# Weight preparation software-pipelined by three chunks, and moved behind the first projection

## The reference, cut to what matters

```python
# x: (32, 2048, 1024) fp32; four batches to a core
xn = layernorm(x)
x + attn(xn) + ffn(xn)

def attn(xn):                       # 16 heads of 64
    q, k, v = xn @ Wq + bq, xn @ Wk + bk, xn @ Wv + bv
    q_freq, k_freq, v_freq = rfft over the sequence of q, k, v
    idx = top 64 frequencies by mean |q_freq|
    score = sum(q.real * k.real) / 8 at idx;  attn = softmax(score)
    out_freq = mean over frequencies of q_freq, with attn * v.real put at idx
    return irfft(out_freq) @ Wo + bo

def ffn(xn):                        # int32 weights, scale 1/127, hidden 3072
    return (silu(xn @ wg.T) * (xn @ wu.T)) @ wd.T
```

## Time and profile before

| what | us |
|---|---|
| three timed runs | 5865.82, 5973.41, 6274.16 |
| their median | 5973.41 |
| the profiled execution's own time | 5865.05 |
| its span (slowest core, first to last instruction) | 5863.5 |
| the spans of its 8 cores | 5843.6 to 5863.5 |
| TensorE busy | 4717.2 (80%) |
| VectorE, ScalarE, GpSimd busy | 1368.9, 837.2, 60.7 |

### The profile page before, as it was taken

One profiled execution on the slowest core, in us unless ns is written; L12 is line 12 of the kernel. 1 busy time (PEld: TensorE's weight loads), 2 busy tenths in 40 slices (PEclk: granted clock), 3 DMA queues, 4 the chain that ended last, 5 costly groups with the idle time before them and its releaser, 6 DMA issues.

```text
span 5863.5 us, 52343 instructions; the slowest of 8 cores (5843.6 to 5863.5 us)
## 1 busy us (share of the span) xinstructions
PE 4717.2 (80%) x20720; PEld 1989.3 (34%) x20720; DVE 1368.9 (23%) x1819; ACT 837.2 (14%) x976; POOL 60.7 (1%) x116
## 2 busy tenths in 40 slices
PE   0157468899885898799995799789987599889989
PEld 0023123344332333234442343234433243324434
DVE  1113023112122322202222232302222332221212
ACT  1111011122101111022201111112200111112210
POOL 0000000000000000000000000000000000000000
PEclk9778778999996999899997799899998799989999
DMA  3232222122341211222242211213233031212234
GB/s 98 86 90 79 75 61 72 42 85 76 110 126 52 61 44 36 76 68 77 63 154 85 47 44 46 66 56 88 76 120 121 29 72 44 55 51 81 79 99 124
DMA packets 570711, 441.87 MB, mean 75 GB/s; under 512 B 276940, under 2 KB 473676, under 8 KB 570472
## 3 DMA queue, kind: packets, MB, share of 16 engines
q1 hardware_dynamic: 548712, 360.92, 22.2%
q0 software_dynamic: 12544, 44.05, 2.3%
q10 hardware_dynamic: 9216, 33.56, 1.4%
HBM read 373.46 MB, written 65.01 MB: 75 GB/s over the span
## 4 chain that ended last, share of the span: by engine, by line
PE 75%; DMA 13%; DVE 6%; issue 3%; ACT 2%; DVEq 0%; ACTq 0%; SPq 0%; POOLq 0%
PE pw L587 14%; PE pw L917 11%; PE pw L926 11%; PE pw L958 11%; PE pw L469 8%; PE pw L541 4%; PE pw L827 4%; PE pw L860 4%; DMA strm<-wq_s 1%; PE pw L477 1%; DMA strm<-wv_s 1%; DMA r<-wdT_s 1%; PE pw L631 1%; DMA wdT_s<-spE 1%; DVE msum L499 1%
## 5 line engine op out<-in xcount | busy, mean ns | idle before, releaser
L587 PE MATMUL pw<-r,strm 128*128 128x512 bf16 x4096 | 922.7, 389 | 195.7 <-ACT r L595 156.3
L917 PE MATMUL pw<-r,strm 128*128 128x512 bf16 x3072 | 703.2, 382 | 36.2 <-ACT strm L901 36.2
L469 PE MATMUL pw<-strm,r 128*128 128x512 bf16 x2304 | 541.5, 388 | 211.8 <-ACT r L481 188.1
L926 PE MATMUL pw<-r,strm 128*128 128x512 bf16 x3072 | 694.4, 379 | 0.0
L587 PEld LDWEIGHTS pw<-r,strm 128*128 128x128 bf16 x4096 | 407.8, 100 | 709.0 <-issue 250.4
L958 PE MATMUL pw<-r 128*128 128x512 bf16 x2048 | 459.9, 383 | 63.3 <-DMA r<-wdT_s 63.3
L936 DVE TENSOR_TENSOR r<-strm,pw 128x1024 bf16<-128x1024 bf16 x192 | 234.5, 1221 | 1036.1 <-PE pw L926 1036.1
L917 PEld LDWEIGHTS pw<-r,strm 128*128 128x128 bf16 x3072 | 302.4, 99 | 406.3 <-issue 50.0
L926 PEld LDWEIGHTS pw<-r,strm 128*128 128x128 bf16 x3072 | 300.6, 98 | 362.5
L469 PEld LDWEIGHTS pw<-strm,r 128*128 128x128 bf16 x2304 | 216.3, 99 | 527.2 <-issue 300.7
L933 ACT ACTIVATE strm<-pw 128x1024 bf16<-128x1024 f32 x192 | 196.6, 1024 | 1015.2 <-PE pw L917 1015.1
(11 more groups left out here) (173 smaller groups left out, 2662.1 us busy)
## 6 DMA issues: line engine op xcount, KB each, us to landing
strm<-dft_cos SPq DMA_DIRECT2D x96, 512.0 KB
r<-x SPq DMA_DIRECT2D x64, 512.0 KB
spA<-wg SPq DMA_DIRECT2D x48, 512.0 KB
spC<-wu SPq DMA_DIRECT2D x48, 512.0 KB
spB<-wg SPq DMA_DIRECT2D x48, 512.0 KB
spD<-wu SPq DMA_DIRECT2D x48, 512.0 KB
strm<-dft_sinn SPq DMA_DIRECT2D x32, 512.0 KB
r<-crt SPq DMA_DIRECT2D x8, 2048.0 KB
```

What stands on the lines that cost most here:

```text
L469: e.matmul(pw[pwi][:, eta * 512:(eta + 1) * 512], xnT[:, dc, tau * 128:(tau + 1) * 128], wv[:, dc, eta * 512:(eta + 1) * 512], start=(dc = ...
L587: e.matmul(pw[pwi][:, eta * 512:(eta + 1) * 512], slotv[:, tau, :], sig[:, tau, eta * 512:(eta + 1) * 512], start=(tau == 0), stop=(tau == ...
L917: e.matmul(pw[pg][:, tq * 512:(tq + 1) * 512], wgv[:, dc, :], xnT[:, dc, th * 1024 + tq * 512:th * 1024 + (tq + 1) * 512], start=(dc == 0) ...
L926: e.matmul(pw[pu][:, tq * 512:(tq + 1) * 512], wuv[:, dc, :], xnT[:, dc, th * 1024 + tq * 512:th * 1024 + (tq + 1) * 512], start=(dc == 0) ...
```

## The change

It has two parts. First, `prep_one` still emits the load at once, but puts cast and store of the chunk on a list; when the list holds more than three, the oldest pair is emitted. So the cast and the store of chunk i are emitted behind the load of chunk i + 3. `prep_flush` emits the last three pairs at the end of each weight of eight chunks and of each group of twelve. The fences stay: POOL still waits for every DMA to land before it issues the next. Second, the preparation of Wk and Wv is emitted after the first projection and not before it.

```diff
+    prep_pipe = []
...
         em("g", lambda e, it=it, src_ap=src_ap:
            e.dma_start(out=it, in_=src_ap), writes=SP4[par], dma=True)
-        em("v" if i % 2 == 0 else "s", lambda e, it=it, ph=ph, i=i:
-           (e.tensor_copy if i % 2 == 0 else e.copy)(spEh[ph], it),
-           reads=SP4[par], writes=[f"spE{ph}"])
-        em("g", lambda e, ph=ph, dst_ap=dst_ap: e.dma_start(out=dst_ap, in_=spEh[ph]),
-           reads=[f"spE{ph}"], writes=[dtk], dma=True)
+
+        def cast_store(i=i, it=it, par=par, ph=ph, dst_ap=dst_ap, dtk=dtk):
+            em("v" if i % 2 == 0 else "s", lambda e, it=it, ph=ph, i=i:
+               (e.tensor_copy if i % 2 == 0 else e.copy)(spEh[ph], it),
+               reads=SP4[par], writes=[f"spE{ph}"])
+            em("g", lambda e, ph=ph, dst_ap=dst_ap: e.dma_start(out=dst_ap, in_=spEh[ph]),
+               reads=[f"spE{ph}"], writes=[dtk], dma=True)
+
+        prep_pipe.append(cast_store)
+        if len(prep_pipe) > 3:
+            prep_pipe.pop(0)()
+
+    def prep_flush():
+        while prep_pipe:
+            prep_pipe.pop(0)()
 
     def prep_attn(nm):
         for dc in range(8):
             prep_one(W_ins[nm][dc * 128:(dc + 1) * 128, :],
                      w_scr[nm][dc * 128:(dc + 1) * 128, :], f"scr{nm}", False)
+        prep_flush()
...
         prep_state["i"] = min(i0 + n, len(ffn_chunks))
+        prep_flush()
...
             phase_ln(b)
+            phase_proj(b, 0)
             prep_attn("Wk")
             prep_attn("Wv")
-            phase_proj(b, 0)
             prep_attn("Wo")
```

## The result

Over ten runs each, the changed kernel takes 0.9866 of the time of the kernel before (95% interval 0.9853 to 0.9880): a small gain, clear of the noise. This ratio leaves out the runs in which one die was granted a lower clock, which the medians over all ten, 5843.0 and 5871.13 us, mix in. The forecast was 5781 / 5865.05 = 0.9857. The profiled execution took 5789.06 us, its span is 5787.5 (before 5863.5): 76.0 us less, where the sum gave 84.1.

What follows compares the result with a forecast made beforehand. TensorE, 80% busy, was taken to stand still behind POOL's weight preparation, whose casts precede the PSUM evictions. Terms -17.3 - 14.4 - 26.2 - 26.2 = -84.1 us against 5865.05 gave 5781 us, range 5757 to 5885.

Steps and rivals of the forecast that it cites:

- the sum: Forecast gains of Step 1, Step 2 and the two wd groups of Step 3 added: -84.1 us.
- The cost of a chunk: On POOL: store 2.88 us plus load 4.42 us to next issue, a period of 7.30 instead of 8.28 us.
- The restart: PE goes on after a preparation stall 1.7 us after the last-but-one store of the group is issued.
- Step 1: Wq preparation before the layernorm: 22.3 us won, less contention with SP's loads, net -17.3 us.
- Step 2: First projection matmul to PE's restart in the transform with Wq: 229.3 instead of 243.7 us, net -14.4.
- Step 3: Two groups of 12 wd chunks: 65.9 us, the second 4.7 more, net -26.2 us each.
- A: Likeliest case: gains as worked out, 5781 us, by itself 5765 to 5800; chance 0.60.
- B: Rival: casts and neighbouring DMAs hold each POOL load back, leaving 5795 to 5812 us; chance 0.22.
- C: Rival: first 850 us come out without any losses and loads take 4.2 us, giving 5757 us; chance 0.14.
- D: Rival: slower, POOL's chain of 24 chunks behind the projection with loads over 6.5 us; at 7 us, 5884; chance 0.04.
- The sign of being wrong: On POOL's timeline, a load taking above 5 us to the next issue would show the forecast wrong.
- The other two signs: An x load after 95 us; a span after the second wd group not some 84 us shorter but changed elsewhere.

Runs made afterwards that it cites:

- Experiment 6: Changed kernel with the chunks of Wk, Wv, Wo and wd spread over the stages, still pipelined: 0.9507 of the kernel before, span 5554.4 us.
- Experiment 5: Changed kernel with the first Wk load held back until the first layernorm tile is transposed: span 5782.0 us, 5.5 below the changed kernel.
- experiment 7: Kernel of Experiment 6 with cast and store directly behind each load again: span 5572.3 us, 17.9 above it.
- Experiment 4: Changed kernel without table loads for the first four frequency blocks of the transform with Wq: 6231 us at lower clocks, only first 600 us compared.
- experiment 1: Changed kernel with the move undone, so the pipelining alone: 0.9812 of the kernel before, profiled execution 5764.59 us.
- experiment 2: Kernel before with the move alone, no pipelining: ratio 1.0056, span 5887.1 us, 23.6 above the kernel before.
- experiment 3: Changed kernel with all 56 casts of the preparation on DVE, none on ACT: span 5730.5 us, 57.0 below the changed kernel.

## Why the prediction was right, point by point

**What bounds the kernel** was right: POOL's chain of load, cast and store ahead of the evictions. Experiment 6, which leaves the DMAs and the casts as they are and only moves them among the other work, takes the stalls away.

**The cost of a chunk** was right. Load to next issue was put at 4.42 us from rows that did not show it. The changed kernel's POOL in the middle of Wv:

```profile
319.13 0.53 POOL L384 DMA_DIRECT2D spA<-Wv  x1 [2.32 <-DMA wv_s<-spE]
323.65 0.55 POOL L390 DMA_DIRECT2D wv_s<-spE  x1 [3.98 <-DMA spA<-Wv]
326.52 0.53 POOL L384 DMA_DIRECT2D spB<-Wv  x1 [2.32 <-DMA wv_s<-spE]
```

4.52 and 2.87 us, a period of 7.39. In Wq, Wv, Wo and the first wd group it is 7.3 to 7.4 on average; beside table loads it is 9.7 (Wk, four periods) and 7.7 (second wd group). The 40 loads on the path take 4.64 us on average. The bridge of landing plus 0.55 us, the step seen behind a cast, was sound. The restart, put at 1.7 us behind the last-but-one store, came at 1.75 (411.67 - 409.92).

**Step 1** was 1.9 us too good. The first store came 2.7 us late (25.55 against 22.84; 2 taken), first to last store took 38.3 us (37.8), and the Wq reads with the step to x 25.6 (21.9 now, 3 taken, 3.7 measured). Experiment 5 shows that the last is POOL's Wk loads. The first store waits for a DVE cast that stands behind the four bias casts, and the last of these starts at 23.71 us against 21.00 before; SP's read of bv, issued at 17.81 beside a Wq load, is followed by the next one only 4.26 us later (2.31 before). Without the pipelining (experiment 7) the first store is issued at 23.17. So loads beside the bias reads are the likely reason, but no run took them away with the pipelining in place.

**Step 2** was 4.0 us too good, and the term that was mis-sized is the table loads: 5.5 us were taken over from Wo's chunks, and the first four periods alone took 38.87 us where 29.2 was their price, 9.7 more. Experiment 4 removes 7.4 of it. In experiment 1, where the table loads meet Wo's chunks, the first four periods take 38.28 us: the place does not matter. In experiment 2, where they meet Wk's chunks without the pipelining, the first five periods take 48.1 us, 6.7 above five of 8.28. Without it POOL's queue stands idle behind the casts for part of the time; with it the queue is denser, and the same eight table loads meet more of it. That fits these three numbers but is argued, not shown. That the move alone loses 23 us was right (25.4, experiment 2); with the pipelining it loses 37.9 (experiment 1), which the forecast had not worked out: it priced the move on the kernel before, where one load of Wo is covered by the projection, not four. The whole sum was right all the same, since step 2 priced the new order as it stands. But of the two parts of the change only the first was a gain.

**Step 3** was right: 66.5 and 69.3 us where 65.9 and 70.6 were forecast. Two small terms between the groups were not in the sum: +1.1 us in the transform and +1.4 in the projection, which is the first tile after the stall (6.53 us against 5.13). The 7.7 us between the two sums are 1.9 of step 1, 4.0 of step 2 and these 2.5, less 0.7 that step 3 won. Most of steps 1 and 2 is contention between queues, for which A had left room in its own range (5765 to 5800); the measured 5789 lies in it.

**The rivals.** B's mechanism exists (experiment 3), but its price of 0.69 us on half the loads does not occur, as the casts end too early in the issue. The forecast had the cast start just under the next load issue, which it does (0.38 us ahead of it), but did not work out that it then ends 0.22 us before the issue. Nor are all POOL issues of the kernel before 0.53 to 0.55 us: the first load of all takes 0.67. Of C nothing came. D needed 6.5 us a load; one load on the path passed that. POOL's timeline of the changed kernel, beside the table loads:

```profile
251.28 0.53 POOL L384 DMA_DIRECT2D spA<-Wk  x1 [2.70 <-DMA wk_s<-spE]
257.93 0.55 POOL L390 DMA_DIRECT2D wk_s<-spE  x1 [6.12 <-DMA spA<-Wk]
262.55 0.53 POOL L384 DMA_DIRECT2D spB<-Wk  x1 [4.07 <-DMA wk_s<-spE]
```

This load takes 6.65 us to the next issue and this store 4.62; the three loads after it take 5.3 to 6.0, and behind them those of this chain take 4.3 to 4.6. The move's loss, with which D began, was there, and the pipelining covered it.

**The sign of being wrong** "load to next issue above 5 us" came true for six of the 40 loads on the path: these four and two of the second wd group (5.20 and 6.21), all beside table loads. The other two signs did not come: the first x load is at 91.90, and nothing has grown or shrunk elsewhere (4650 us against 4652 in the last stretch). The forecast had counted about ten such neighbours and priced them at the 5.5 and 4.7 us seen before.

## What to carry to other kernels

Before pipelining a preparation that makes an engine wait, look at where its work stands in the in-order streams: here 48 casts cost TensorE 239 us of waiting because they stood in groups ahead of the evictions, and the same casts one at a time between the evictions cost almost nothing. Once they are spread, the pipelining gains nothing in the spread part that these runs can tell from zero. Work moved behind a stage no longer runs beside it: price the move by itself, with the rest of the change already in place; here it cost 38 us of what the pipelining had won. Loads that nobody waits for are not free when another queue runs on the critical path beside them.

## What the runs showed of the hardware

- A DMA issue of GpSimd is held by a VectorE cast from fp32 or int32 to bf16 (0.69 us) until about 0.12 us after the cast's end: it took 0.78 or 0.79 us where the cast began 0.03 us before it. Where the cast began 0.38 us before it, and so ended 0.31 us into it, it took its usual 0.53 us, and the next DMA followed after 4.3 to 4.5 us.
- Two queues with one DMA each in flight slow each other: beside table loads of 512 KB a load of that size took up to half as long again (5.3 to 6.65 us instead of 4.4), and a store up to 4.62 instead of 2.88; beside four such loads, eight reads of 256 KB with the step to the next load took 25.6 us instead of 20.4.
- In experiment 1 two of eight cores (0 and 1) were granted a clock of 0.80 in a transform in which core 2 had 1.00, after a stall of 10.3 against 13.7 us; the 384 matmuls took 102.14 us on core 0 and 85.75 in the changed kernel. In experiment 6, without stalls, the cores' clocks over the span were 0.920 to 0.924 against 0.904 to 0.907 in the changed kernel.
